# Queries projected 512 columns at a time in the two wide attention layers, and unsplit probabilities and values in the third layer

## The reference, cut to what matters

```python
# third attention (L2): 32 query heads of 128, 4 key/value heads; keys are context and latents, 128 per sequence
hidden = concatenate([context, latents], axis=1)
q = (latents @ Wq).reshape(b, q_len, 4, 8, 128)
k, v = (hidden @ Wk, hidden @ Wv)              # reshaped to (b, 128, 4, 128)
attn = softmax(einsum('bqhgd,bkhd->bhgqk', q, k) / sqrt(128))
out = einsum('bhgqk,bkhd->bqhgd', attn, v).reshape(b, q_len, 4096) @ Wo
# fourth attention (L3): 32 query heads of 128, 8 key/value heads, 64 keys, causal
q, k = _rope(x @ Wq.T), _rope(ctx @ Wk.T)
ctx = softmax(where(causal, q k^T * scale, min)) @ v
out = ctx @ Wd.T                                # (4096 -> 512)
```

## Time and profile before

| What | Value |
|---|---|
| median of 3 runs | 1805.06 us (1804.2 to 1806.93) |
| the profiled execution, whole | 1810.68 us |
| its span, first to last instruction | 1808.9 us |
| PE busy | 1594.0 us (88%), 10450 instructions |
| DVE, ACT, POOL busy | 952.2 us (53%), 698.4 us (39%), 628.2 us (35%) |
| mean granted PE clock | 0.948 |

### The profile page before, as it was taken

The page is one execution under the profiler, slowest core; times in us unless marked ns, Lnnn a source line. Parts: engine busy times, 40 slices in busy tenths (PEclk is TensorE's granted clock), DMA queues, the critical chain, the costliest instruction groups (busy, mean ns, idle before and its releaser), DMA issues. The chain is left out here.

```text
span 1808.9 us, 29350 instructions
## 1 busy us (share of the span) xinstructions
PE 1594.0 (88%) x10450; PEld 1330.0 (74%) x10450; DVE 952.2 (53%) x1857; ACT 698.4 (39%) x2015; POOL 628.2 (35%) x594
## 2 busy tenths in 40 slices
PE   5887879859699999999999996968999999999976
PEld 4655666548588988888888895757778877877853
DVE  4885668777424322331432326686565656655653
ACT  3443154344335435443452533442333234224221
POOL 2542244475313212321331321334343534434410
PEclk9997999969899999999999999879999999999986
DMA  5001110021301100110000001231112112211001
GB/s 193 1 1 47 40 37 1 1 85 52 85 27 48 36 24 25 44 39 19 30 24 24 25 24 54 98 88 59 59 35 74 54 35 81 70 54 39 13 3 47
DMA packets 27865, 81.14 MB, mean 45 GB/s; under 512 B 3248, under 2 KB 11952, under 8 KB 22768
## 3 DMA queue, kind: packets, MB, share of 16 engines
q1 hardware_dynamic: 26896, 79.44, 13.2%
q10 hardware_dynamic: 864, 0.30, 0.1%
HBM read 69.25 MB, written 10.49 MB: 44 GB/s over the span
## 5 line engine op out<-in xcount | busy, mean ns | idle before, releaser
L386 PE MATMUL bank<-hid_high,wq_high 128*128 128x256 f32 x1152 | 343.6, 298 | 6.5 <-DVE probs_last L1181 5.8
L386 PE MATMUL bank<-hid_low,wq_high 128*128 128x256 f32 x1152 | 327.1, 284 | 0.0
L386 PE MATMUL bank<-hid_high,wq_low 128*128 128x256 f32 x1152 | 327.0, 284 | 0.0
L386 PE MATMUL bank<-wo_high,out_high 128*128 128x512 f32 x576 | 241.5, 419 | 43.5 <-DVE out_low L1231 37.6
L1239 DVE SCALAR_TENSOR_TENSOR x_stream<-bank,gates,x_stream 128x512 f32<-128x512 f32 x128 | 96.1, 751 | 266.6 <-PE bank L386 266.6
L386 PEld LDWEIGHTS bank<-hid_high,wq_high 128*128 128x128 f32 x1152 | 221.9, 193 | 14.4 <-issue 10.1
L386 PE MATMUL bank<-wo_low,out_high 128*128 128x512 f32 x576 | 230.8, 401 | 0.0
L386 PE MATMUL bank<-wo_high,out_low 128*128 128x512 f32 x576 | 229.8, 399 | 0.0
L1025 POOL TENSOR_TENSOR probs_middle<-probs_middle,small 128x512 f32<-128x512 f32 x64 | 66.7, 1042 | 458.4 <-DVE small L1226 458.4
L386 PEld LDWEIGHTS bank<-hid_low,wq_high 128*128 128x128 f32 x1152 | 222.3, 193 | 2.9 <-issue 2.9
L386 PEld LDWEIGHTS bank<-hid_high,wq_low 128*128 128x128 f32 x1152 | 221.8, 193 | 0.0
(11 more groups left out here) (255 smaller groups left out, 3504.2 us busy)
## 6 DMA issues: line engine op xcount, KB each, us to landing
raw_q<-in_L_wq SPq DMA_DIRECT2D x18, 1024.0 KB, 5.1
raw_o<-in_L_wo SPq DMA_DIRECT2D x18, 1024.0 KB, 4.9
values_last<-ctx_values SPq DMA_DIRECT2D x32, 256.0 KB, 3.9
values_t_last<-ctx_keys SPq DMA_DIRECT2D x8, 512.0 KB, 5.3
raw_c<-in_L_wkv SPq DMA_DIRECT2D x6, 512.0 KB, 5.3
x_stream<-in_x SPq DMA_DIRECT2D x8, 256.0 KB, 9.8
ctx_keys<-raw_o SPq DMA_DIRECT2D x8, 256.0 KB, 2.0
ctx_values<-raw_o SPq DMA_DIRECT2D x16, 128.0 KB, 2.4
```

What stands on the lines that cost most here:

```text
L386: last = k.nc.tensor.matmul(out, stationary(a, c), moving(b, c), start=n == 0, stop=n == total - 1)
```

## The change

1. A query product is now one head for half of the sequences: `half, head = divmod(q, 4)`, 12 instructions of 512 columns. There are still eight per unit.
2. A half of the tokens has its own buffer for each of the four heads. In the middle layer these are `queries_t` and a new `queries_t2`; in the last layer the second half lies in the upper part of `values_t` and in `raw_c`, so the next stage's load into `raw_c` now waits for the last scores of the layer.
3. `scores(t)` waits for all four heads of its half: `q` = 0 to 3 before slot 0, `q` = 4 to 7 before slot 4.
4. `AHEAD` is 4: four products before the unit (slots 7 to 10, or slot 11), four in slots 0 to 3. The split of the next query weights moves to slot 4 (ACT) and slots 4 and 5 (POOL).
5. In the last layer DVE's key rotation stands ahead of `update(t - 3)`.
6. In the middle layer probabilities and values are no longer split: `value_low` and `probs_low` are gone, and `attend` issues one plain fp32 instruction where there were three of `fp32r`.

```diff
             self.e, self.vt = sb("probs", 4 * 512), sb("values_t", 1024)
-            self.pt = [sb("probs_t_high", 1024, F32R), sb("probs_t_low", 1024, F32R)]
-            self.vj = [sb("values_high", 2048, F32R), sb("values_low", 2048, F32R)]
+            self.pt, self.vj, self.q2 = sb("probs_t", 1024), sb("values", 2048), sb("queries_t2", 2048)
         else:
...
     scale = float(P) ** -0.5
-    Q = k.q[:].rearrange("p (a h n) -> p a h n", a=2, h=4)
-    Q2 = k.q[:].rearrange("p (a g b h n) -> p a g b h n", a=2, g=2, b=4, h=2)
+    if rope:
+        Q = [[k.q[:, D * i:D * i + D] for i in range(4)],
+             [k.vt[:, 1024 + D * i:1024 + D * i + D] for i in range(2)] + [k.raw_c[:, D * i:D * i + D] for i in range(2)]]
+    else:
+        Q = [q[:].rearrange("p (g b h n) -> p g b h n", g=2, b=8, h=2) for q in (k.q, k.q2)]
     RING = 5 if rope else 4
...
     if rope:
-        KV_AT, BACK_AT, Q_AT = {}, {}, {8: [0], 9: [1], 10: [2]}
+        KV_AT, BACK_AT, Q_AT = {}, {}, {7: [0], 8: [1], 9: [2], 10: [3]}
     else:
-        KV_AT, BACK_AT, Q_AT = {6: [0], 7: [1], 8: [2, 3], 9: [4, 5], 10: [6, 7]}, {10: [0, 1], 11: [2, 3]}, {11: [0, 1, 2]}
+        KV_AT, BACK_AT, Q_AT = {6: [0], 7: [1], 8: [2, 3], 9: [4, 5], 10: [6, 7]}, {10: [0, 1], 11: [2, 3]}, {11: [0, 1, 2, 3]}
     SLOTS = T + LAG + (1 if rope else 2)
-    AHEAD = 3
+    AHEAD = 4
...
             if rope:
-                fetch_ahead(k, sp, NEXT[f"L{layer}"], "c")
                 load_keys(0)
...
                         load_values(j, half)
+                fetch_ahead(k, sp, NEXT[f"L{layer}"], "c", k.s_psum, k.at("s_psum", 8 * kv_heads))
             else:
...
                 else:
-                    r = n - NT
-                    if r >= 4:
-                        pool.wait_ge(k.s_psum, v("s_psum", j, 8 * UN, 2 * (r // 2) - 2))
-                    out = Q[:, (r // 2) % 2, 2 * (r % 2):2 * (r % 2) + 2, :].rearrange("p h n -> p (h n)")
+                    half, head = divmod(n - NT, 4)
+                    pool.wait_ge(k.s_psum, v("s_psum", j, 8 * UN, 4 * half - 4))
+                    out = Q[half][head]
                 nc.gpsimd.tensor_tensor(out, TMP[:, n % 2], TMP2[:, n % 2], ALU.add).then_inc(k.q_sbuf, 1)
...
                             low_c(j + 1)
-                        if t in (5, 6) and not (last and u == UN - 1):
-                            low_q(j, u + 1, 2 * (t - 5), 2 * (t - 5) + 2)
+                        if t in (4, 5) and not (last and u == UN - 1):
+                            low_q(j, u + 1, 2 * (t - 4), 2 * (t - 4) + 2)
                 if rope and not last:
...
                 act.wait_ge(k.vt_psum, v("vt_psum", j, NT, n + 1))
-                nc.scalar.copy(V[0][:, 512 * n:512 * n + 512], k.bank[2 + n % 2][:]).then_inc(k.v_hi, 1)
+                nc.scalar.copy(V[0][:, 512 * n:512 * n + 512], k.bank[2 + n % 2][:]).then_inc(k.v_sbuf, 1)
             def queries(j, u, q):
-                p, h = divmod(q, 2)
-                act.wait_ge(k.q_psum, v("q_psum", j, 8 * UN, 8 * u + 2 * p + h + 1))
-                nc.scalar.activation(Q2[:, p % 2, h].rearrange("p b h n -> p h b n"),
-                                     k.bank[4 + h][:].rearrange("p (h b n) -> p h b n", h=2, b=4), ACT.Copy,
+                half, head = divmod(q, 4)
+                act.wait_ge(k.q_psum, v("q_psum", j, 8 * UN, 8 * u + q + 1))
+                nc.scalar.activation(Q[half][:, head // 2, :, head % 2, :],
+                                     k.bank[4 + q % 2][:].rearrange("p (b n) -> p b n", b=8), ACT.Copy,
                                      scale=scale).then_inc(k.q_sbuf, 1)
...
                             high_c(j + 1)
-                        if t == 5 and not (last and u == UN - 1):
+                        if t == 4 and not (last and u == UN - 1):
                             high_q(j, u + 1)
...
                                     value_back(j + 1, n)
-                        if t >= T and not rope and u < UN - 1:
-                            queries(j, u + 1, t - T)
+                        if t >= T - 1 and not rope and u < UN - 1:
+                            queries(j, u + 1, t - T + 1)
                         if LAG <= t < T + LAG:
...
-                    def probs_low(t):
-                        dve.wait_ge(k.pt_hi, v("pt_hi", j, 8 * UN, 8 * u + t + 1))
-                        nc.vector.tensor_tensor(PT[1][:, t % 2], k.bank[2 + t % 2][:], PT[0][:, t % 2],
-                                                ALU.subtract).then_inc(k.pt_sbuf, 1)
                     ahead = u == UN - 1 and not last
...
                             queries(j, t + AHEAD)
-                        if not rope and LAG <= t < T + LAG:
-                            probs_low(t - LAG)
+                        if rope and 6 <= t < 6 + NT and not last:
+                            key(j + 1, t - 6)
                         if ahead:
                             for q in part(Q_AT, t, 0):
                                 queries(j + 1, q)
-                            for n in () if rope else part(BACK_AT, t, 0):
-                                value_low(j + 1, n)
                         if LAG + 1 <= t <= T + LAG:
...
                                 ln_variance_vector(k, dve, tile // 2, tile // 2 + 2)
-                        if rope and 6 <= t < 6 + NT and not last:
-                            key(j + 1, t - 6)
                         if ahead:
                             for q in part(Q_AT, t, 1):
                                 queries(j + 1, q)
-                            for n in () if rope else part(BACK_AT, t, 1):
-                                value_low(j + 1, n)
                         if LAG <= t < T + LAG:
...
             def queries(j, u, q, first=False):
-                p, h = divmod(q, 2)
+                half, head = divmod(q, 4)
                 if rope:
-                    if p:
-                        pe.wait_ge(k.rope_mul, v("rope_mul", j, ROPES, NT + 2 * p + h - 1))
+                    if q >= 2:
+                        pe.wait_ge(k.rope_mul, v("rope_mul", j, ROPES, NT + q - 1))
                     elif not first:
-                        pe.wait_ge(k.rope_mul, v("rope_mul", j, ROPES, h - 1))
+                        pe.wait_ge(k.rope_mul, v("rope_mul", j, ROPES, q - 1))
                     if q == 0:
                         pe.wait_ge(k.lo_q, v("lo_q", j, 4 * UN, 4))
-                elif p or u:
-                    pe.wait_ge(k.q_sbuf, v("q_sbuf", j, 8 * UN, 8 * u + 2 * p + h - 1))
+                elif q >= 2 or u:
+                    pe.wait_ge(k.q_sbuf, v("q_sbuf", j, 8 * UN, 8 * u + q - 1))
                 else:
-                    pe.wait_ge(k.kv_sbuf, v("kv_sbuf", j, 2 * NT, 2 * NT - 1 + h))
+                    pe.wait_ge(k.kv_sbuf, v("kv_sbuf", j, 2 * NT, 2 * NT - 1 + q))
                     pe.wait_ge(k.lo_q, v("lo_q", j, 4 * UN, 4))
-                for i in (2 * h, 2 * h + 1):
-                    last_mm = product(k, k.bank[4 + h][:, 256 * (i % 2):256 * (i % 2) + 256],
-                                      lambda s, c: k.wq[s][:, c * D + i * P:c * D + (i + 1) * P],
-                                      lambda m, c: hid_cols(k, m, c, 4 * p, 4, 1), C)
-                last_mm.then_inc(k.q_psum, 1)
+                product(k, k.bank[4 + q % 2][:], lambda s, c: k.wq[s][:, c * D + head * P:c * D + (head + 1) * P],
+                        lambda m, c: hid_cols(k, m, c, 8 * half, 8, 1), C).then_inc(k.q_psum, 1)
...
                 queries(0, 0, 2)
+                queries(0, 0, 3)
             else:
...
                     def scores(t):
-                        p = t // 2
+                        half = t // 4
                         if rope:
-                            pe.wait_ge(k.q_sbuf, v("q_sbuf", j, ROPES, NT + 2 * p + 2))
+                            pe.wait_ge(k.q_sbuf, v("q_sbuf", j, ROPES, NT + 4 * half + 4))
                         else:
-                            pe.wait_ge(k.q_sbuf, v("q_sbuf", j, 8 * UN, 8 * u + 2 * p + 2))
+                            pe.wait_ge(k.q_sbuf, v("q_sbuf", j, 8 * UN, 8 * u + 4 * half + 4))
                         if rope:
                             pe.wait_ge(k.max_ready, v("max_ready", j, 8 * UN, 8 * u + t))
                             for i in range(4):
                                 for c in range(2):
-                                    rows, tok = slice(S * c, S * c + S), P * (t % 2) + S * c
+                                    rows, tok = slice(S * c, S * c + S), P * (t % 4) + S * c
                                     last_mm = nc.tensor.matmul(k.bank[6][rows, i * S:(i + 1) * S],
-                                                               Q[:, p % 2, i, tok:tok + S],
+                                                               Q[half][i][:, tok:tok + S],
                                                                k.kt[:, t * P + S * c:t * P + S * c + S],
...
                                 b, cols = 2 * t + i, slice(256 * i, 256 * i + 256)
```

(24 more changed lines are left out.)

3 lines of the change are left out of this document (1 added, 2 removed).

## The result

| | before | after |
|---|---|---|
| median of four runs each | 1805.69 us | 1786.82 us (1785.37 to 1788.5) |
| ratio, 95% interval | | 0.9896 [0.9879, 0.9913] |
| profiled execution / its span | 1810.68 / 1808.9 us | 1788.5 / 1786.7 us |
| mean granted PE clock | 0.948 | 0.954 |

The kernel became 19 us faster, 3 us more than forecast, and inside the range. Six more runs of it beside another experiment gave 1789.38 us, ratio 0.9911 [0.9892, 0.993]. But the total hides two errors of opposite sign: the middle layer was forecast at +0.7 us and brought about -9, the last layer was forecast at -16.2 and brought about -9. That they cancelled is luck.

What follows compares the result with a forecast made beforehand. Both layers were taken as bound by PE's instruction count and the spacing of starts, with stalls worth removing only in the last. Middle +0.7 and last -16.2 gave -15.5 us, so 1790 us; own range 1784 to 1796, 8 in 10: 1780 to 1803.

Steps and rivals of the forecast that it cites:

- Width: Both layers: 128 query products of 512 instead of 256 columns save 0.10 us each, 12.8 us in all.
- first rival: Both layers: width buys nothing because the striped read has its price per column; 1803 us, chance 0.13.
- Unsplit: Middle layer: plain fp32 `attend` 10.2 us more, slot 2's wait for `probs_low` 5.5 less, other dropped DVE work worth nothing.
- More uncovered slots in the middle layer: Middle layer: seven more projection waits for `out_low` in slots without a query product, 0.34 us each, 2.4 us more.
- third rival: More is won: 0.12 us per product, shorter waits in slots 4 to 6, half the gate's price; 1779 us, chance 0.17.
- (a): Last layer: key rotation in DVE's idle time and slot 7's product cut the 2.06 us wait to 0.57; 10.4 us less.
- (b): Last layer: five half-clock stretches behind the long waits vanish, 1.6 us each, 8.0 us less.
- fourth rival: Last layer: the clock still falls, behind the 0.9 us gate or the 3.7 us start; 1798 us, chance 0.12.
- (d) and (e): Last layer: scores 0 wait for `q` = 3, 0.9 us in seven units (6.3 more), and 3.7 us before the first.
- second rival: Last layer: rotation finds DVE and POOL busy at 15 gates, PE waits 2.7 us more each; 1831 us, chance 0.10.
- (c): Last layer, slot 1: the wait of scores 2 for the rotated `q` = 3 goes, 0.25 us each, 2.0 us less.
- (f): Last layer, last unit: no product ahead, so one uncovered slot more, 0.6 us more.

Runs made afterwards that it cites:

- experiment 4: Changed kernel with each query product issued as 24 instructions of 256 columns, all else kept: 1809.54 us, ratio 1.0034 to the kernel before.
- experiment 2: Kernel before with only the middle layer's values and probabilities unsplit (plain fp32): 1808.23 us, ratio 1.0008.
- experiment 3: Changed kernel with the middle layer's probabilities and values split again: 1788.73 us, ratio 0.9912 to the kernel before.
- 9: Changed kernel with query-weight low parts all in slot 4, one gate per head in the last layer, middle layer split again: 1779.64 us, ratio 0.9857.
- experiment 5: Changed kernel with DVE's key rotation back behind update(t - 3) in the last layer: 1801.04 us, ratio 0.9979 to the kernel before.
- experiment 1: Changed kernel with the old function for the last layer, so only the middle layer changed: 1796.64 us, ratio 0.9944.
- the repeat (10): Changed kernel run once more, unaltered: 1789.38 us, ratio 0.9911 to the kernel before.

## Why the prediction was right, and where it was not

The direction, the size and the likeliest case came out; the forecast's own range (1784 to 1796) held the time. But the prediction gave a sign of its own for being wrong, a middle layer that changes by more than 5 us, and it changed by 9.4. So its account of the middle layer is wrong, and the total is right by luck. The steps:

- **Width.** Forecast 12.8 us, 0.10 per product. Measured 0.11 to 0.13 per product (experiment 4; the earlier trace rows against 2.82 and 2.86 after give 0.10 to 0.13), some 14 us, and experiment 4 makes it 20 to 23 in all. The term was mis-sized for two reasons. I took the lower of two rows. And I counted only the distance between PE's instructions, not that they have to be fetched: "issue" waits of 1.4 and 2.0 us at two turns of the loop, 2.4 us of which are gone, and the stretch at half clock that followed one of them (841.1 to 844.5 us in the kernel before, 1.6 us). That row stood in the same view as the earlier trace rows, and the prediction passed over it. That width buys nothing (first rival) is refuted. So is, for this kernel, the size estimated from the Trainium skill, "TensorE: Matmul & The Clock Gate", section "Back-to-back issue gap": the estimate was 4 us. The page gives that formula for an isolated instruction, not for a stream of weight loads and matrix instructions as here. (The sum of 1803 that the first rival takes from it is off by 1: six instructions at 109 ns make 64 `attend` 2.9 us dearer than forecast, not 4.)
- **Unsplit.** Forecast +10.2 - 5.5 + 0 = +4.7. Measured +8.3 for `attend` and -7.1 with the transposes, the waits behind them and the change from one kind of instruction to the other; by ratio, unsplitting costs 1.4 us in experiment 2 and saves 0 to 3 in 3 and 9, none of them told apart from zero. `attend` itself was as forecast, 0.87. The sum is smaller because the last one of each of the first seven units, which has a product behind it, costs 0.67 for 0.71 before and not 0.15 more. Of the -7.1, 5.8 are the wait in slot 2, 1.40 to 0.68 in eight units; the rest may be that between transposes and `attend` no change of kind remains, which the forecast gave no price and no run tests by itself.
- **More uncovered slots in the middle layer.** Forecast +2.4, measured no more waiting in sum: the waits for `out_low` went from 6.3 to 5.2 us. The slots do cost something, 0.5 us unsplit (4.7 in experiment 2, 5.2 after) and 1.1 split (6.3 before, 7.4 in experiment 3), but DVE, without the low parts, is earlier and gives 1.6 to 2.2 back. The third rival had that. The gate at the scores cost 1.7 where I said nothing.
- **Last layer (a),** the key rotation in DVE's idle time: forecast -10.4. The waits for `out_low` fell by 11.7, and experiment 5 shows that the order did it. But in the same place 4.0 us came up for `wq_low`, which is the one missing step: I asked what DVE would do in its idle time and not what POOL was doing in it. A full-clock unit was forecast 1.64 us shorter (0.80 + 1.49 + 0.25 - 0.90) and is 1.07 shorter (64.00 to 62.93); the difference is the 0.58.
- **(b) The clock.** Forecast -8.0. The five slow stretches inside the units are gone, worth 1.22 to 1.40 us a unit rather than 1.6, since the transposes with their wait are 0.2 shorter in those units than in the others; with 0.2 at the start of the first unit that is 6.8 in all. A stretch at half clock behind the wait of 3.6 us gives 1.4 back. Net -5.4. The fourth rival was thus right at the start of the layer and nowhere else. The windows view of the changed kernel (columns of the earlier trace rows):

```profile
1230.80:1234.20 3.40, 3.08 (x21) 2.58 (x22) 0.84 (x2) 1.00 (x6) 0.19 (x1) 0.50 0.00 0
1451.00:1484.00 33.00, 31.14 (x188) 24.11 (x186) 23.32 (x36) 7.10 (x25) 14.29 (x12) 1.00 0.20 58
```

- **(d) and (e), the gates.** Forecast 0.9 and 3.7 us, measured 1.01 and 3.60. The gate at slot 4 was priced at nothing and costs 0.17 in seven units, 1.2 us. The chain of product's end, three rotations, one addition was priced well. The second rival (long gates) is refuted; its threshold of 1.0 us more per gate was never near.
- **(c)** holds: the product in slot 1 with what follows takes 2.94 to 2.95 us where it took 3.21. **(f)** can't be told apart in the ledger.

So the step that failed is the middle layer's sum. Against its terms the ledger has 1.4 us more for width, 1.9 less cost for `attend`, 1.6 more at the transposes, -1.1 instead of +2.4 at the projections, and 2.4 for the loop's turn, which had no term; with 0.7 the other way that is the 10.1 us between +0.7 and -9.4. The last layer's missing 7.5 us, chiefly the wait for `wq_low` (4.0), the clock (2.6) and the gate at slot 4 (1.2), with width 0.6 the other way, nearly cancelled it.

## What to carry to other kernels

Where PE is bound by how many instructions it issues, price a wider instruction twice: by the distance between starts, and by the fetch of instructions, which shows as "issue" waits where a loop jumps back. When work is moved into an engine's idle time, look at what the other engines do there: the slot was idle for DVE and busy for POOL, and the two slowed each other, since DVE's operands both lay in SBUF. And give a gate the finest condition that the consumer can use; one wait for four heads cost 0.4 us a unit more than four waits for one.

## What the runs showed of the hardware

- DVE and POOL slow each other when DVE has both operands in SBUF and POOL works from SBUF too, on fp32: a 64x512 multiplication of DVE 0.69 to 1.01 and 1.68 us, two subtractions of 128x512 on POOL 2.52 to 3.41, a 128x256 multiplication of POOL 0.61 to 0.97 and 1.06. With one of DVE's operands in PSUM they don't: in the last layer of the changed kernel 39 multiplications of 64x512 from `bank` ran for more than half of their time beside POOL and took 0.68 to 0.69, and in experiment 5, where the key rotation is out of the way, POOL's multiplication takes 0.60 to 0.62 throughout.
- A chain of 12 matrix instructions of 512 columns takes 0.11 to 0.13 us less from its start to the next piece's than one of 24 of 256 columns; stripes of 64 columns out of 128 carry no price of their own beside the key product's 2.85.
- Instructions that must be fetched can stop PE where a loop jumps back: two waits of 1.4 to 2.0 us in each of three kernels that fetch the loop's code again in each pass (17 or 18 packets on q8 from 690 to 985 us), none in those that fetch it once (none). How long the loop may be before this happens, no run measures; none kept the wide products and lengthened the code by as much.
- A wait of about 2 us does not always bring the half clock: of seven waits of 2.06 to 2.10 us in the kernel before five were followed by it, of the same seven in experiment 1 four, of seven of 1.97 in experiment 5 one. What decides stays open. One of 1.81 us in the last unit was followed by it in the repeat (10) and in experiment 4, and not in the first profile of the changed kernel. None of the waits of 1.01 us and less in the last layer's units was.
